# A decoder layer on one core: most of the recurrence moved into the FFN stage, silu from ScalarE's table, FFN units on all eight PSUM banks

## The reference

```python
x = layernorm(x + attn(x))                 # 16 heads of 32, causal mask of -10000
x = layernorm(x + wkv(w, u, k=x, v=ctx))   # a recurrence along the tokens, per channel
x = layernorm(x + ffn(x))                  # silu(x Wg^T) * (x Wu^T), then Wd^T; width 2048

# wkv, written without the running maximum: with ek = exp(k),
#   p[t+1] = exp(w) p[t] + ek[t] v[t]      q[t+1] = exp(w) q[t] + ek[t]
#   y[t]   = (p[t] + exp(u) ek[t] v[t]) / (q[t] + exp(u) ek[t])
```

## Time and profile before

| | us |
|---|---|
| median of 3 runs | 837.43 |
| lowest, highest | 837.21, 839.4 |
| the profiled execution's own time | 835.81 |
| its span, from first to last instruction | 834.0 |
| TensorE busy in it | 743.1 |
| VectorE busy | 558.8 |
| ScalarE busy | 408.3 |
| GpSimd busy | 271.2 |
| mean granted clock of TensorE | 0.959 |

### The profile page before, as it was taken

The page is one execution under the profiler, slowest core; times in us unless marked ns, Lnnn a source line. Parts: engine busy times, 40 slices in busy tenths (PEclk is TensorE's granted clock), DMA queues, the critical chain, the costliest instruction groups (busy, mean ns, idle before and its releaser), DMA issues.

```text
span 834.0 us, 11936 instructions
## 1 busy us (share of the span) xinstructions
PE 743.1 (89%) x4256; PEld 404.1 (48%) x4256; DVE 558.8 (67%) x1217; ACT 408.3 (49%) x1000; POOL 271.2 (33%) x284
## 2 busy tenths in 40 slices
PE   5988699978889978999677598889999999999997
PEld 2555456644456545565443254434454444444443
DVE  4455545778998879998898488874774544344434
ACT  5568767777567776686846213302332034104310
POOL 2001233328341155500346515541622133103320
PEclk9999799998999989999979899999999999999999
DMA  7246494232034122141620610001000100010001
GB/s 248 62 138 217 139 215 127 89 114 65 13 89 139 44 72 77 33 117 56 133 44 1 101 51 1 1 13 39 2 1 13 38 1 1 14 38 1 1 13 38
DMA packets 44331, 54.17 MB, mean 65 GB/s; under 512 B 4720, under 2 KB 33648, under 8 KB 44272
## 3 DMA queue, kind: packets, MB, share of 16 engines
q1 hardware_dynamic: 41008, 47.11, 18.0%
q0 software_dynamic: 3264, 6.29, 4.4%
HBM read 47.10 MB, written 12.58 MB: 72 GB/s over the span
## 4 chain that ended last, share of the span: by engine, by line
PE 59%; DVE 18%; issue 6%; POOL 6%; ACT 5%; DMA 3%; SPq 3%; POOLq 0%; DVEq 0%; ACTq 0%
PE psb L717 20%; PE psb L607 7%; PE psb L730 6%; PE psb L728 6%; PE psb L697 5%; PE psb L654 4%; DVE ek L1034 4%; DVE ee L946 3%; PE psb L621 2%; SPq L1270 2%; PE psb L643 2%; DMA xt<-in_xT 2%; PE psb L665 2%; PE psb L704 1%; PE psb L633 1%
## 5 line engine op out<-in xcount | busy, mean ns | idle before, releaser
L946 DVE CUSTOM_DVE_ANT_0 ee<-psb,mask,clip 128x512 f32<-128x512 f32 (+3 forms) x256 | 131.0, 530 | 54.7 <-PE psb L643 54.1
L810 ACT ACTIVATE ee<-ee,nm 128x512 f32<-128x512 f32 (+3 forms) x256 | 142.8, 559 | 32.4 <-DVE nm L946 32.1
L654 PE MATMUL psb<-ident,ee 128*128 128x128 f32 x640 | 108.5, 288 | 25.9 <-ACT ee L821 25.7
L821 ACT ACTIVATE ee<-psb 128x512 f32<-128x512 f32 (+1 forms) x192 | 100.0, 521 | 56.4 <-PE psb L654 56.1
L1212 POOL TENSOR_TENSOR hl<-hf,hh 128x512 f16<-128x512 f32 x64 | 77.5, 1211 | 134.9 <-ACT hh L884 134.9
L884 ACT ACTIVATE hh<-hf 128x512 bf16<-128x512 f32 x64 | 40.4, 632 | 144.1 <-DVE hf L1059 144.1
L717 PE MATMUL psb<-x2h,wg 128*128 128x512 f16 x256 | 99.5, 389 | 6.6 <-DVE th L1049 5.9
L654 PEld LDWEIGHTS psb<-ident,ee 128*128 128x128 f32 x640 | 76.3, 147 | 54.2 <-ACT ee L821 34.5
L717 PE MATMUL psb<-x2l,wg 128*128 128x512 f16 x256 | 99.7, 390 | 0.0
L730 PE MATMUL psb<-wd,hl 128*128 128x512 f16 x256 | 97.0, 379 | 2.3 <-POOL hl L1212 2.3
L717 PE MATMUL psb<-x2h,wu 128*128 128x512 f16 x256 | 97.5, 381 | 0.0
(11 more groups left out here) (106 smaller groups left out, 1236.3 us busy)
## 6 DMA issues: line engine op xcount, KB each, us to landing
qs<-parts SPq DMA_DIRECT2D x64, 128.0 KB, 2.7
ks<-parts SPq DMA_DIRECT2D x64, 128.0 KB, 2.9
parts<-qhl SPq DMA_DIRECT2D x16, 256.0 KB, 2.1
parts<-khl SPq DMA_DIRECT2D x16, 256.0 KB, 2.1
x<-in_x SPq DMA_DIRECT2D x4, 1024.0 KB, 7.8
ct<-in_ctxT SPq DMA_DIRECT2D x4, 1024.0 KB, 6.2
out<-x SPq DMA_DIRECT2D x16, 256.0 KB, 2.0
xt<-in_xT SPq DMA_DIRECT2D x14, 256.0 KB, 4.0
```

The lines of the kernel that those rows point to most:

```text
L654: mm = e.transpose(PSB[:, bk, o:o + P], E[H % 3][:, EOFF[i] + j * P:EOFF[i] + (j + 1) * P], IDENT[:])
L810: e.activation(dst, dst, ACT.Exp, bias=NM[:, n % 4, col:col + 1], scale=-1.0, accum_out=DEN[:, n % 4, col:col + 1]).then_inc(sem("exp"), 1)
L821: e.activation(ET[h][:, base:base + width], PSB[:, bank["turn", H, item], 0:width], ACT.Copy).then_inc(sem("et"), 1)
L946: e.tensor_tensor_reduce(E[H % 3][:, EOFF[i]:EOFF[i] + w], PSB[:, bank["score", H, i], 0:w], MASK[:, S - w:S], -SC, CLIP[:, i:i + 1], ALU. ...
```

## The change

- **Recurrence.** Its places are now given one by one. Batch 0 stays (groups 6 and 7). Batch 1 has three chunks in groups 13, 14 and 15, the fourth in iteration 6 of batch 0's FFN; batches 2 and 3 stand in the FFN stage of batches 0 and 1, partly beside the y's (places 16 to 19 of a batch are its y's). yt and x2t of batches 1 to 3 follow there.
- **Buffers.** EK2 and the ctx tile exist twice (batch 2 has the second, CT2), TH and HF three times from unit 4 on. CT2 and the third TH and HF lie where the attention's tiles were.
- **silu.** From unit 4 of batch 0 on `th` is ScalarE's Silu, `aa` is gone, and `hf` has another scale; `th` empties the gate's bank.
- **Banks.** From the end of group 15 on all units take any of the eight banks.
- **Other places.** The early units stand in slots 9 to 15 instead of 6 to 15. Two gate/up units stand between the last turn and the end of attention, one before pv and one after the second spread. wo of batch 3 stands in iterations 8 to 11, the zeros of wd in 7 to 14, and y waits for each row of wd by itself. wo of batch 2 stands in group 12 (six parts) and 13 (six) instead of three and nine. The four loads of wg stand at one slot (6) of group 14 and also wait until k of group 15 is stacked; their zeros stand at slots 2, 4, 6 and 8 of group 15. A y is followed by four ticks instead of two.
- `on_dve`, with COPIES_ON_DVE empty, adds nothing to the program.

```diff
+WKV_AT = {(0, 0): (6, 6), (0, 1): (6, 15), (0, 2): (7, 4), (0, 3): (7, 10), (1, 0): (13, 4), (1, 1): (14, 4), (1, 2): (15, 2)}
+WKV_IN = {(1, 3): (0, 6), (2, 0): (0, 11), (2, 1): (0, 16), (2, 2): (0, 18), (2, 3): (1, 3), (3, 0): (1, 8),
+          (3, 1): (1, 13), (3, 2): (1, 16), (3, 3): (1, 18)}
+YT_IN = {1: ((0, 12), (0, 13), (0, 14), (0, 15)), 2: ((1, 9), (1, 10), (1, 11), (1, 12)), 3: ((2, 6), (2, 7), (2, 8), (2, 9))}
+X2_IN = {1: ((0, 17), (0, 17), (0, 18), (0, 18)), 2: ((1, 16), (1, 17), (1, 17), (1, 18)), 3: ((2, 13), (2, 14), (2, 15), (2, 16))}
+WO_IN, ZERO_IN = (8, 9, 10, 11), 7
-EARLY, E0, YTS, ZPS, WOS, X2S, WGS = 4, 6, 2, 2, 4, 6, 4
+EARLY, E0, YTS, ZPS, WOS, X2S, ZGS = 4, 9, 2, 2, 4, 6, 2
...
-    "gate": lambda b, it: ("aa", b, it),
+    "gate": lambda b, it: ("aa" if early(b, it) else "th", b, it),
...
-                if b + 1 < B:
-                    add("load_ct", b + 1)
+                if b < 2:
+                    add("load_ct", 2 * b + 1)
...
     for k in range(T):
-        at(NG - 2, WGS + 3 * k, "load_f", "wg", k)
+        at(NG - 2, X2S, "load_f", "wg", k)
         at(NG - 2, X2S + 3 * k, "x2t", 0, k)
-        at(NG - 1, k, "zero", "wg", k)
+        at(NG - 1, ZGS + 2 * k, "zero", "wg", k)
...
+        elif b == B - 1:
+            wos = wo_units(b - 1) if g == 0 else wos
+            todo = ([(qs, 4, 10), (wos[:6], 10, 16)], [(wos[6:], 3, 11), (qs, 11, 16)], [])[g]
...
+    tt.pool = ALL
     for k in range(T):
         add("load_f", "wd", k)
     turn(NHG - 1, 2)
+    tick()
+    gu(0, EARLY)
     tt.unit("pv", NG - 1)
...
     spread(NG - 1, 1)
     rest[NG - 1]()
+    gu(0, EARLY + 1)
     tick()
+    add("load_ct", 2)
...
+    for b in range(B):
+        for it in range(0 if b else EARLY + 2, IT):
+            gu(b, it)
+            tick()
+            if b == 0 and 0 <= it - ZERO_IN < IT // 2:
+                add("zero", "wd", 2 * (it - ZERO_IN))
+                add("zero", "wd", 2 * (it - ZERO_IN) + 1)
+            for u in beside.get((b, it), ()):
                 u()
             tick()
...
         for t in range(T):
             y(b, t)
-            tick()
-            tick()
+            for u in beside.get((b, IT + t), ()):
+                u()
+            for _ in range(4):
+                tick()
...
+    def ring(b, it):
+
+        z = b * IT + it
+        return RINGS[z % 2 if z < EARLY else (z - EARLY) % 3]
...
-            pe.wait_ge(*by_zero("wd", IT - 1))
             for it in range(IT):
+                pe.wait_ge(*by_zero("wd", it))
...
-            if z:
-                act.wait_ge(sem("y2"), z)
-            e.activation(EK2[:], src, ACT.Exp, bias=MU2[:, c:c + 1]).then_inc(sem("ek"), 1)
+            if z >= 2:
+                act.wait_ge(sem("y2"), z - 1)
+            e.activation(EK2S[z % 2][:], src, ACT.Exp, bias=MU2[:, c:c + 1]).then_inc(sem("ek"), 1)
...
+            if early(b, it):
+                e.activation(ring(b, it)[0][:], PSB[:, bank["gate", b, it], :], ACT.Tanh,
+                             scale=GT[:, it:it + 1]).then_inc(sem("th"), 1)
+            else:
+                e.activation(ring(b, it)[0][:], PSB[:, bank["gate", b, it], :], ACT.Silu,
+                             scale=G2[:, it:it + 1]).then_inc(sem("th"), 1)
...
-            dve.wait_ge(*by("aa", b, it))
+            dve.wait_ge(*by("aa" if early(b, it) else "th", b, it))
...
             if name == "wg":
+                pool.wait_ge(*by_stack(NG - 1, "k"))
```

More of the change, by code:

```diff
@@ L70, in flush, with unit @@
             self.held_back.pop(0)[1]()
-    def unit(self, *piece, pool=GBANK):
+    def unit(self, *piece, pool=None):
+        pool = pool or self.pool
         def emptied(k):
@@ L86, in unit, with early, on_dve @@
         return k
+def early(b, it):
+    return b == 0 and it < EARLY
+def on_dve(H, item):
+    return item == 0 and H // 4 in COPIES_ON_DVE
 EMPTIED = {
@@ L310, in timetable @@
         at(7, 4 * k + ZPS, "zero", "wu", k)
+    for piece, place in WKV_AT.items():
+        at(*place, "wkv", *piece)
+    for t in range(T):
+        at(8, YTS + (14 - YTS) * t // 3, "yt", 0, t)
     for b in range(B - 1):
[L312 to L317, removed]
         for k in range(T):
@@ L405, in timetable @@
     rest[NG - 1]()
+    gu(0, EARLY + 1)
     tick()
+    add("load_ct", 2)
     wo3 = wo_units(B - 1)
[L408 to L411, removed]
-        tick()
-        if it < 4:
-            for u in wo3[3 * it:3 * it + 3]:
+    beside = {}
+    for piece, place in WKV_IN.items():
+        beside.setdefault(place, []).append(lambda piece=piece: wkv(*piece))
+    for t in range(T):
+        beside.setdefault((0, WO_IN[t]), []).extend(wo3[3 * t:3 * t + 3])
+        for b in range(1, B):
+            beside.setdefault(YT_IN[b][t], []).append(lambda b=b, t=t: yt(b, t))
+            beside.setdefault(X2_IN[b][t], []).append(lambda b=b, t=t: x2t(b, t))
+    for b in range(B):
[6 more added lines that the diff above has]
+            for u in beside.get((b, it), ()):
                 u()
             tick()
[L417 to L424, removed]
-        tick()
[L426 to L437, removed]
         for t in range(T):
             y(b, t)
-            tick()
-            tick()
+            for u in beside.get((b, IT + t), ()):
+                u()
+            for _ in range(4):
+                tick()
     tt.flush()
@@ L473, in build @@
     CT = sb(ctx, "ct", [P, T, S], F32)
[L474 removed]
+    EK, EKV = (sb(ctx, n, [P, S], F32) for n in ("ek", "ekv"))
+    EK2S = [sb(ctx, f"ek2_{k}", [P, S], F32) for k in (0, 1)]
+    G2, C2 = (sb(ctx, n, [P, IT], F32) for n in ("g2", "c2"))
     PS, QS_ = sb(ctx, "ps", [P, S + 1], F32), sb(ctx, "qs_", [P, S + 1], F32)
@@ L578, in by_emptied, with ring_had @@
         return by(*EMPTIED[last[0]](*last[1:])) if last else None
+    def ring(b, it):
+        z = b * IT + it
+        return RINGS[z % 2 if z < EARLY else (z - EARLY) % 3]
+    def ring_had(b, it):
+        z = b * IT + it
+        return max([k + 1 for k in range(z) if ring(0, k) is ring(b, it)], default=0)
     def parts_of(w):
@@ L952, in expand, with turned @@
             e.reciprocal(D2[:, n % 4, :], D2[:, n % 4, :]).then_inc(sem("rec"), 1)
+        def turned(H, item):
+            n, h = divmod(H, 4)
+            base, width = TBASE[item], P * sum(T - j for j in TRI[item])
+            dve.wait_ge(*by("turn", H, item))
+            if n:
+                dve.wait_ge(*by("pv", n - 1))
+            e.tensor_copy(ET[h][:, base:base + width], PSB[:, bank["turn", H, item], 0:width]).then_inc(sem("et2"), 1)
         def t1_t2(n):
@@ L1033, in divide @@
             dve.wait_ge(sem("den"), T * b + c + 1)
-            e.reciprocal(EK2[:, cut], EK2[:, cut]).then_inc(sem("rcp"), 1)
+            e.reciprocal(EK2S[c % 2][:, cut], EK2S[c % 2][:, cut]).then_inc(sem("rcp"), 1)
         def zero(name, k):
```

82 lines of the change are left out of this document (47 added, 35 removed).

## The result

| | before | after |
|---|---|---|
| median of 5 runs, us | 837.29 | 830.91 |
| lowest, highest | 835.05, 839.4 | 829.11, 833.64 |
| span of the profiled execution | 834.0 | 828.8 |
| after to before | | 0.9927 (0.9899 to 0.9955) |

The change saves 6.4 us, 0.7% by the ratio. The forecast was 16 us. The time lies inside the stated range, but only 0.4 of the forecast saving came, so something was mis-sized, and the rest of this text is about that.

A forecast was written before the change was run, and what follows sets the result against it. TensorE was taken to bound the FFN wherever fed and groups 12 and 13, VectorE groups 11 and 15. Attention -6.8 and FFN -9.0 gave -15.8 us: median 821.5, range 809 to 833.

The forecast's parts named there:

- Attention: Groups 10 to 15, with seven recurrences left of twelve: forecast sum -6.8 us, from -13 to +1.
- Group 13 as a wrong place: Attention group 13 gets recurrence (1,0): VectorE, 27.7 us busy, becomes its bound; some 28.7 us, +3.5.
- Group 15: Last attention group, one recurrence instead of three, early units from slot 9: 37.5 us instead of 43.6, -6.
- The transition: Attention's end into FFN: two gate/up units close the 4.33 and 3.85 us holes; 0.5 us kept.
- three stretches at the lower clock: FFN before 556 us: TensorE at about 1.2 GHz after three holes, 1.7 us lost each, 5.0 removable.
- silu priced at nothing on ScalarE: FFN units: up to 19 table loads, 3.9 us per recurrence with the exponentials, claimed hidden behind TensorE.
- a round of five units: FFN, ScalarE's chain for five gate/up units with one recurrence: 12 + 3.9 = 15.9 of TensorE's 17.3 us.
- the upper end (23.1): FFN, silu's cost on ScalarE: ends 0 and, with every VectorE piece serial as well, 23.1 us.
- its slower rival: FFN: ScalarE's order holds it, 5.8 us lost in each of five recurrences, +13, 850 us; chance 0.08.
- the sign that the prediction named: FFN: TensorE waiting for th in batches 1 and 2 would show ScalarE's order holding the FFN.
- The new wait at x2t: FFN, x2t of batch 1 behind the second y: TensorE waits 4 us, then 1.7 at lower clock, +5.7.
- The removed aa: FFN, 60 of 64 units: 41 us off VectorE, worth 0 from 573 us on, makes room in batch 0.

The follow-up runs named there:

- the run without loads: The changed kernel with Tanh in place of Silu in the 60 units, aa still absent, so ScalarE's table never changes; 823.93 us, 0.9825 of before.
- the run with nothing on GpSimd beside the norms: The changed kernel with hh behind the next th, plus recurrences (2,1) and (2,2) each one y later; 816.87 us, 0.9747 of before.

## Why the prediction was wrong

- **Attention: direction right, size short.** Forecast -6.8, measured -10.7 for groups 10 to 15 (-8.8 up to the FFN's first mark): group 11 28.9 us (30.3 forecast), 12 23.0 (24.6), 13 27.9 (28.7), 15 38.4 (37.5), 10 and 14 together 48.5 (49.4). In groups 11 and 12 TensorE's busy time fell by 2.0 and 1.1 us against the earlier trace rows, more than the flips removed explain, and in group 14 it rose by 1.8; over the six groups it fell by 4.3, about the nine flips of 0.44. So work moved between groups, and the single group forecasts were partly lucky.
- **Group 13 as a wrong place: not borne out.** It is as long as forecast, but not for the reason given: VectorE was to be busy 27.7 us in it and was 24.6 of 27.9. In group 12, where VectorE has more room, the same piece costs 7.0 us instead of 5.9. The step compared busy sums; a slot order makes a group longer without any engine full.
- **Group 15:** the size was nearly right, the reason not. It was read as VectorE's total in slots 0 to 8, some 20 us, and the first early unit did start 19.2 us into the group; but it waited for the last zero, and the order of the zeros alone was worth 3.4 us.
- **The transition: right in kind.** 0.91 and 1.47 us stayed instead of 0.5. The sum took three stretches at the lower clock to be removable; there were four, since the clock was down behind the 4.33 us too (0.61 from 465.4 to 469.4 us, 1.6 lost). The 1.47 at wo's wait for ol is gone in the run without loads: it was theirs.
- **silu priced at nothing on ScalarE: this is the step that failed.** The prediction had the loads' length right, 1.28 us, and their count nearly (15 instead of up to 19: two recurrences among the y's share theirs). It summed a round of five units to 15.9 us against TensorE's 17.3 and called it hidden. Measured from hf to hf, the round is 576.53 to 595.36, 18.8 us, against 17.7 without loads (576.17 to 593.87), which is TensorE's own, five units and a flip. What the sum left out is that VectorE stands idle during the loads and has the recurrence's 7 us to do after them, in series. The prediction had this as the upper end (23.1) and as its slower rival, with 0.08, and said that y's and banks would hide it. They hid part: 9.5 us came through, not 29, and not as a wait for th in the units, the sign that the prediction named, but mostly as a wait for hh in the first y of batch 1. So the term of the sum that failed is the 0 us for the loads, which measured 9.5 of the missing 10.7: without them the FFN length is 359.1, the forecast 357.9. That it comes so near is in part luck. In the run without loads the transition, the holes in the y's and the new wait each measured more than forecast, some 4 us together, and the fourth stretch at the lower clock that went was worth 1.6 the other way.
- **What a switch of the table takes.** The rows show a switch as the load of 1.28 us with the next activation 0.02 us behind it. The Trainium skill (ScalarE: Activation LUTs, What ACT_TABLE_LOAD costs) adds a drain for 2.66 us in all; no such time shows in these rows, and the measurement decides. The same page's rule (Table sets) is to batch calls by set. The trace agrees that alternating costs here, 9.5 us for 15 loads; silu with its loads still came out ahead of tanh with aa by 3.7.
- **The new wait at x2t: right, a little short.** Forecast 4 us and 1.7 at the lower clock, measured 5.88 and (3.4 x 0.47 =) 1.6. From the yd of the first y to the end of the norms VectorE took 13.0 us, 11 forecast. The norms were priced at 2.24 and took 3.73 beside GpSimd. The Trainium skill (SBUF — State Buffer, SBUF: two separate sides) says that VectorE, where it uses both its pairs of ports, and GpSimd take the shared pair in turn, for a whole instruction. The 1.91 us in the run with nothing on GpSimd beside the norms agree with sharing; that one waits for a whole instruction of the other is not shown here.
- **The removed aa** was given its worth in batch 0 alone, none from 573 us on. It is worth 13.2 us with no loads (10.5 by the medians), and 8.3 of them are lost in batch 1, from 563 us on, with a hole of 4.93 in its first y. Wrong: that TensorE never waited for aa there was read from the layout before, which had one recurrence in batch 1, not five.
- **The gap in the first y of batch 1** was in no part of the prediction; it is where the loads' lag, a recurrence and slow norms meet. The norms alone do not make it: they take 4.58 us in the run without loads too, and the hole there is 0.65.

Open: whether exponentials made in one go for several recurrences would save loads wasn't tried.

## What to carry to other kernels

A switch of ScalarE's table is not paid in ScalarE's busy time but in the chain in which it stands: count what each engine does not do while it waits, and issue the next function of the same table ahead of the step that waits for another engine. Before moving a piece by busy sums, look at what is queued behind it on its engine; a norm or a zero placed too late on VectorE cost 3 to 8 us here, and reordering alone brought 17 us. An edit that frees an engine is worth what the layout lets it be worth: silu cost 6 us in the old layout and gained 4 in the new. Which difference of the two layouts decides that, banks, buffers or places, was not taken apart.

## What the runs showed of the hardware

Four norms of 128 x 512 on VectorE took 1.91 us alone and 3.73 and 4.57 beside GpSimd's operations on two tiles. A table load took 1.28 us each of 16 times, with the next activation 0.01 or 0.02 us behind it where nothing else was waited for. After holes of 5.88 and 4.92 us TensorE ran at about half its clock for some 3.5 us, after the one of 4.53 for some 5.5; after one of 1.40 and one of 2.26 it didn't, and after 2.17 in the kernel before it did. After the same two holes of 1.47 and 0.51 us it did in one profile and not in another, so the length of a hole alone does not tell. The start of a run, up to the end of group 0, varied by 2 us with no change in that part of the kernel.
